# Sums written in the place of their low parts, a spare region in their stead, and two first images with orders of their own

## What is computed

```python
# x: 32 images, 256 channels, 28 x 28
xp  = log_pooling(x)                     # 12 averages over bins of a 9 x 9 neighbourhood, (2 levels x 6 angles)
out = conv(xp, w_conv1, stride=(4, 3))   # 256 -> 256 channels, one weight for each of the 12 averages
out = out + conv(x, w_center, 1 x 1) + b_center
mean, var = over images and places, per channel
out = (out - mean) * rsqrt(var + 1e-5) * gamma + beta
return relu(out + x)
```

## Time and profile before

| | us |
|---|---|
| median of 3 runs | 1634.29 |
| lowest, highest | 1633.83, 1634.32 |
| the profiled execution | 1634.39 |
| its span | 1632.7 |
| TensorE busy | 1459.9 (89%) |
| DVE busy | 1421.4 (87%) |
| ACT busy | 639.6 (39%) |
| GpSimd busy | 121.3 (7%) |
| data moved | 268.76 MB |

### The profile page before, as it was taken

The page is one execution under the profiler, slowest core; times in us unless marked ns, Lnnn a source line. Parts: engine busy times, 40 slices in busy tenths (PEclk is TensorE's granted clock), DMA queues, the critical chain, the costliest instruction groups (busy, mean ns, idle before and its releaser), DMA issues.

```text
span 1632.7 us, 22865 instructions
## 1 busy us (share of the span) xinstructions
PE 1459.9 (89%) x8468; PEld 1458.6 (89%) x8468; DVE 1421.4 (87%) x1391; ACT 639.6 (39%) x689; POOL 121.3 (7%) x160
## 2 busy tenths in 40 slices
PE   6899999999999999999999999999999999992000
PEld 5899999999999999999999999999999999992000
DVE  7999999999999999999999999999999999986332
ACT  3334434334334343443433334343343333435332
POOL 1000000000000000000000000000000000000000
PEclk8999999999999999999999999999999999996555
DMA  6456554555555555455545555555555455579999
GB/s 200 108 132 146 136 134 126 125 145 127 119 124 133 145 136 137 128 122 143 135 115 120 136 139 136 141 127 128 135 136 122 116 140 133 136 253 420 425 425 400
DMA packets 65352, 268.76 MB, mean 165 GB/s; under 512 B 7616, under 2 KB 7616, under 8 KB 65344
## 3 DMA queue, kind: packets, MB, share of 16 engines
q1 hardware_dynamic: 39744, 160.53, 29.5%
q0 software_dynamic: 20736, 82.45, 26.5%
q10 hardware_dynamic: 4864, 25.69, 3.8%
HBM read 218.07 MB, written 50.58 MB: 165 GB/s over the span
## 4 chain that ended last, share of the span: by engine, by line
PE 86%; DMA 6%; DVE 3%; ACT 2%; another core or an unknown queue 1%; issue 1%; ACTq 0%; SPq 0%; DVEq 0%; POOLq 0%
PE acc L676 29%; PE acc L677 29%; PE acc L675 29%; DMA out<-phase 3%; DMA phase<-y_dram 2%; ACT phase L444 1%; DMA row<-x_wide 1%; DVE pooled L452 1%; DVE pooled_split L453 1%; DVE inner_split L453 0%; ACTq L447 0%; ACT m_copy L403 0%; DVE y_stage L452 0%; DVE row3v L452 0%
## 5 line engine op out<-in xcount | busy, mean ns | idle before, releaser
L387 ACT ACTIVATE pooled_split<-pooled 128x1456 fp32r<-128x1456 f32 x192 | 273.4, 1424 | 609.6 <-DVE pooled L452 609.6
L453 DVE TENSOR_TENSOR pooled_split<-pooled,pooled_split 128x1456 fp32r<-128x1456 f32 x192 | 315.1, 1668 | 0.3 <-ACT pooled_split L387 0.3
L675 PE MATMUL acc<-pooled_split,w_first 128*128 128x364 f32 x768 | 252.7, 329 | 5.1 <-DVE pooled_split L453 5.1
L676 PE MATMUL acc<-pooled_split,w_first 128*128 128x364 f32 x768 | 253.4, 330 | 0.0
L677 PE MATMUL acc<-pooled_split,w_first 128*128 128x364 f32 x768 | 253.4, 330 | 0.0
L677 PE MATMUL acc<-pooled_split,w_outer 128*128 128x364 f32 x768 | 252.8, 329 | 0.0
L676 PE MATMUL acc<-pooled_split,w_outer 128*128 128x364 f32 x768 | 252.5, 329 | 0.0
L675 PE MATMUL acc<-pooled_split,w_outer 128*128 128x364 f32 x768 | 252.0, 328 | 0.0
L675 PE MATMUL acc<-inner_split,w_first 128*128 128x392 f32 (+1 forms) x640 | 219.2, 342 | 13.6 <-DVE inner_split L453 9.3
L677 PE MATMUL acc<-inner_split,w_first 128*128 128x392 f32 (+1 forms) x640 | 218.3, 341 | 0.0
L676 PE MATMUL acc<-inner_split,w_inner 128*128 128x392 f32 (+1 forms) x640 | 218.0, 341 | 0.0
(11 more groups left out here) (82 smaller groups left out, 2154.9 us busy)
## 6 DMA issues: line engine op xcount, KB each, us to landing
row<-x_wide SPq DMA_DIRECT2D x64, 558.0 KB, 3.6
row<-x_wide POOLq DMA_DIRECT2D x64, 558.0 KB, 7.3
ends<-x_wide SPq DMA_DIRECT2D x64, 504.0 KB, 4.0
ends<-x_wide POOLq DMA_DIRECT2D x64, 504.0 KB, 5.8
x_pad<-x SPq DMA_DIRECT2D x64, 392.0 KB, 3.1
y_dram<-y_stage SPq DMA_DIRECT2D x31, 784.0 KB, 8.5
phase<-y_dram SPq DMA_DIRECT2D x30, 784.0 KB, 30.8
out<-phase ACTq DMA_DIRECT2D x30, 784.0 KB, 34.4
```

The lines of the kernel that those rows point to most:

```text
L387: nc.scalar.activation(view(pooled_split, 2 * j * PAIR, (1, PAIR)), view(pooled, (PAIRS * c + j) % 2 * PAIR, (1, PAIR)), ACT.Copy)\
L453: sub = lambda out_, a, b: nc.vector.tensor_tensor(out_, a, b, ALU.subtract)
L675: nc.tensor.matmul(place, hi_w, hi_in, start=start, stop=False)
L676: nc.tensor.matmul(place, lo_w, hi_in, start=False, stop=False)
```

## The change

`inner` and `pooled` are given up. Their sums are written into `phase2` at `INNER_LOW` and `POOLED_LOW`, which are the low halves of `inner_split` and `pooled_split`, and the low part is taken in place. So DVE now waits, ahead of each sum, until TensorE has used the low part of the slice before (`pooled_place`, `inner_done`); ACT's waits for the same go. A region `spare` of the same size as the two buffers is put behind `w_stage`, so that all other buffers move and the total stays.

The first three places of phase two are fetched earlier: place 0 after image 29, places 1 and 2 after image 30. The places within `w_stage` and `spare` are 7 instead of 4, and those up to `w_first` 12 instead of 9. The load of the next x waits for the differences too.

DVE's order is now three: `first_image`, in which each group of weights stands just ahead of its use and each low part right behind its sum; `second_image`; and `image_steps` for the loop, in which columns and boxes come first, then the differences, two pooled sums, and only then the low parts of the inner sums. The warm-up has 70 matmuls.

```diff
--- before.py
+++ after.py
@@ -86,6 +86,8 @@
                 return phase1.enter_context(nc.sbuf_tensor(name, [P, size], dt))
 
             w_stage = reused("w_stage", CH * RAW * CHANNELS)
+
+            spare = reused("spare", 2 * PAIR + 4 * HALF)
             w_first = reused("w_first", 2 * TAPS * CHANNELS, F32R)
             row2 = reused("row2", (W + 3) * ROW2_H)
             row3 = reused("row3", (W + 2) * ROW3_H)
@@ -94,8 +96,6 @@
             box3 = reused("box3", (W + 2) * BOX3_H)
             ends = reused("ends", W * ENDS_H)
             d03 = reused("d03", 2 * U * TALL)
-            inner = reused("inner", 4 * HALF)
-            pooled = reused("pooled", 2 * PAIR)
             INNER = 6 * HALF
             inner_split = reused("inner_split", 2 * INNER, F32R)
             w_inner = reused("w_inner", 2 * INNER_TAPS * CHANNELS, F32R)
@@ -108,6 +108,9 @@
 
         D1, D2, VD, SD = 0, HALF, 2 * HALF, 4 * HALF
 
+        INNER_LOW = start_of["inner_split"] + INNER
+        POOLED_LOW = start_of["pooled_split"] + PAIR
+
         def w_part(c, lo, tap):
 
             if c == 0:
@@ -127,9 +130,9 @@
         def places_within(name):
             return end_of[name] // PLACE
 
-        AFTER_STAGE = places_within("w_stage")
+        AFTER_STAGE = places_within("spare")
         AFTER_FIRST = places_within("w_first")
-        AFTER_SUMS = places_within("pooled")
+        AFTER_SUMS = places_within("d03")
         AFTER_INNER = places_within("w_inner")
         AFTER_PAIR = (start_of["pooled_split"] + 2 * 2 * PAIR) // PLACE
         ALL_PLACES = 2 * (SLOTS - 1)
@@ -212,7 +215,7 @@
         relu_done = sem("relu_done")
         stored = [sem(f"stored{d}") for d in range(SLOTS)]
 
-        WARM_UP = 20
+        WARM_UP = 70
         KINDS = 2
         MOMENTS = KINDS * CH
 
@@ -292,16 +295,17 @@
                 wait_from_one(sp, pooled_ready, PAIRS * s)
                 begin_sum(image, c, ends, W, ends_begun)
 
-            def load_weights(c):
-                for part, (first, end) in enumerate(((0, RAW_OUTER), (RAW_OUTER, RAW))):
-                    sp.dma_start(view(w_stage, (c * RAW + first) * CHANNELS, (1, (end - first) * CHANNELS)),
-                                 w_raw[:, c, first:end, :].rearrange("p k o -> p (k o)"))\
-                        .then_inc(w_loaded[c][part], 16)
+            def load_weights(c, part):
+                first, end = ((0, RAW_OUTER), (RAW_OUTER, RAW))[part]
+                sp.dma_start(view(w_stage, (c * RAW + first) * CHANNELS, (1, (end - first) * CHANNELS)),
+                             w_raw[:, c, first:end, :].rearrange("p k o -> p (k o)"))\
+                    .then_inc(w_loaded[c][part], 16)
 
             def image_steps(image, first=False, last=False):
                 for c in range(CH):
                     if not last:
                         sp.wait_ge(row3_ready, CH * image + c + 1)
+                        sp.wait_ge(v_ready, CH * image + c + 1)
                         load_x(image + 1, c)
                     if c == 0:
                         begin_sums(image, 1)
@@ -324,20 +328,29 @@
                     (load_tail_x if k % 2 else load_tail_y)(0, 1 + k // 2)
 
             load_x(0, 0)
-            load_weights(0)
-            begin_sums(0, 0)
+            load_weights(0, 0)
+            begin_sum(0, 0, row2, W + 3, row2_begun)
+            load_weights(0, 1)
+            begin_sum(0, 0, ends, W, ends_begun)
             load_x(0, 1)
-            load_weights(1)
+            load_weights(1, 0)
+            load_weights(1, 1)
             for dst, src in ((bias, b_center), (gam, gamma), (bet, beta)):
                 sp.dma_start(dst[:, :], src).then_inc(params_loaded, 16)
             image_steps(0, first=True)
-            with sp.Fori(1, LAST) as image:
+            with sp.Fori(1, LAST - 2) as image:
                 image_steps(image)
+
+            image_steps(LAST - 2)
+            sp.wait_ge(w_lo_ready, CH * len(GROUPS))
+            sp.wait_ge(y_saved, 16 * (LAST - 3))
+            load_places(0, 1)
+            image_steps(LAST - 1)
+            load_places(1, 3)
             image_steps(LAST, last=True)
 
             sp.wait_ge(y_saved, 16 * LAST)
-            sp.wait_ge(w_lo_ready, CH * len(GROUPS))
-            load_places(0, AFTER_STAGE)
+            load_places(3, AFTER_STAGE)
             sp.wait_ge(pooled_done, PAIRS * (CH * IMAGES - 1))
             load_places(AFTER_STAGE, AFTER_FIRST)
             sp.wait_ge(pooled_lo_ready, PAIRS * CH * IMAGES)
@@ -373,19 +386,17 @@
 
             def split_inner(s):
                 act.wait_ge(v_ready, s + 1)
-                wait_from_one(act, inner_done, s)
-                nc.scalar.activation(view(inner_split, 0, (1, SD)), view(inner, 0, (1, SD)), ACT.Copy)\
+                nc.scalar.activation(view(inner_split, 0, (1, SD)), view(phase2, INNER_LOW, (1, SD)), ACT.Copy)\
                     .then_inc(inner_hi_ready, 1)
 
                 nc.scalar.activation(view(inner_split, SD, (HALF, 2), (H, U), (1, H)),
                                      view(d03, 2, (U * TALL - 2, 2), (TALL, U), (1, H)), ACT.Copy)\
                     .then_inc(inner_hi_ready, 1)
 
-            def split_pooled(s, c, j):
-                wait_from_one(act, pooled_done, PAIRS * s - PAIRS + j + 1)
+            def split_pooled(s, j):
                 act.wait_ge(pooled_ready, PAIRS * s + j + 1)
                 nc.scalar.activation(view(pooled_split, 2 * j * PAIR, (1, PAIR)),
-                                     view(pooled, (PAIRS * c + j) % 2 * PAIR, (1, PAIR)), ACT.Copy)\
+                                     view(phase2, POOLED_LOW + 2 * j * PAIR, (1, PAIR)), ACT.Copy)\
                     .then_inc(pooled_hi_ready, 1)
 
             def copy_m1(image):
@@ -413,19 +424,17 @@
                     split_inner(s)
                     if c == 1 and not first:
                         measure(image - 1, 1)
-                    if first and c == 0:
-                        split_weights(0, range(FIRST_OUTER_GROUP - 1, len(GROUPS)))
-                        split_weights(1, range(len(GROUPS)))
+                    if first:
+                        split_weights(c, range(len(GROUPS)))
                         act.wait_ge(warmed_up, 1)
                     for j in range(PAIRS):
-                        split_pooled(s, c, j)
+                        split_pooled(s, j)
                     if c == 0 and not first:
                         measure(image - 1, 0)
 
             act.wait_ge(zeroed, 1)
             nc.scalar.activation(std[:, :], std[:, :], ACT.Sqrt)
             act.wait_ge(zeroed, ZEROED)
-            split_weights(0, range(INNER_GROUPS))
             image_steps(0, first=True)
             with act.Fori(1, IMAGES) as image:
                 image_steps(image)
@@ -531,102 +540,157 @@
...
+            def pooled_place(s, j, first, *dims):
+                wait_from_one(dve, pooled_done, PAIRS * s - PAIRS + j + 1)
+                return view(phase2, POOLED_LOW + 2 * j * PAIR + first, *dims)
...
+                add(pooled_place(s, j, 0, (PAIR // 2, 2), (h, 2 * u), (1, h)),
...
+            def differences(image, c):
+                s = CH * image + c
+                dve.wait_ge(x_loaded[c], 16 * (image + 1))
+                wait_from_one(dve, inner_lo_ready, 2 * s)
...
+                wait_from_one(dve, inner_done, s)
+                add(view(phase2, INNER_LOW + D1, *striped), even, odd)
+                sub(view(phase2, INNER_LOW + D2, *striped), odd, even)
...
+            def three_columns(image, c):
+                s = CH * image + c
+                dve.wait_ge(x_loaded[c], 16 * (image + 1))
+                dve.wait_ge(row2_ready, 16 * (s + 1))
...
+            def first_image():
+
+                for c in range(CH):
+                    differences(0, c)
+                    transform_weights(c)
+                    lo_of_sums(c)
+                    lo_of_weights(c, range(INNER_GROUPS))
+                    lo_of_shifted(c)
+                    three_columns(0, c)
+                    boxes(c)
+                    first_sum(c)
+                    lo_of_weights(c, [FIRST_OUTER_GROUP - 1])
+                    lo_of_pooled(c, 0)
+                    second_sum(c)
+                    lo_of_weights(c, range(FIRST_OUTER_GROUP, len(GROUPS)))
+                    lo_of_pooled(c, 1)
+                    third_sum(c)
+                    lo_of_pooled(c, 2)
+
+            def second_image():
+
+                for c in range(CH):
+                    s = CH + c
+                    differences(1, c)
+                    if c == 0:
+                        take_middle(0)
+                    lo_of_sums(s)
+                    three_columns(1, c)
+                    if c == 0:
+                        take_y(0)
+                    lo_of_shifted(s)
+                    boxes(s)
+                    first_sum(s)
+                    lo_of_pooled(s, 0)
+                    second_sum(s)
```

(45 more changed lines are left out.)

90 lines of the change are left out of this document (43 added, 47 removed).

## The result

The changed kernel takes 1646.11 us (median, 1645.95 to 1646.98), the kernel before 1634.1 us on the same chip: a ratio of 1.0075 with an interval of 1.0057 to 1.0092. The forecast was 1645.3. The profiled execution has a span of 1644.4 us against 1632.7, so 11.7 us have to be found.

What follows compares the result with a forecast made beforehand. DVE was taken to bound the start, TensorE the loop at 22.63 us a slice, bytes the end phase. 1634.4 + 16.3 (start) - 5.7 (early places) + 0.3 (contention) = 1645.3 us, range 1639 to 1663.

Steps and rivals of the forecast that it cites:

- The loop stays at 22.63 us: Loop: TensorE's matmuls are unchanged, so each slice (half an image's channels) stays at 22.63 us, with 0.4 us of slack.
- The walk through images 0 and 1: DVE's first four slices, added step by step: done at 35.9, 65.7, 93.2 and 121.5 us, 11.7 us later than before.
- Row2 ahead of slice 4: Switch to the loop's order: DVE waits 0.9 us for row2, and TensorE starts slice 4 at 136.3 instead of 121.87.
- the term for the lower clock: Slice 4, after TensorE's gap: 3.4 us at the low clock level cost 1.5 us.
- The split of the loss: Start of the kernel: 9.8 us of loss from the switch to the loop's order, 4.6 from waits on ACT's copies.
- 70 warm-ups: Start: fifty more warm-up matmuls change nothing; TensorE's later waits for DVE cover their 0 to 0.7 us by slice 2.
- In place: DVE in the loop: taking the low part in place costs the same as from a separate buffer.
- Row2 in the loop: Loop: row2's accumulating half lands in about 7 us, within the 8.3 allowed, so no loss.
- The rival itself: Row2 lands too late in the loop, up to 17.5 us lost, 1663 or any part of it; chance 0.18.
- The end: End phase: three places fetched early gain 5.7 us; only bytes moved ahead count, other places coming free earlier bring nothing.
- the 0.3 for contention: Last image: early fetches compete with row2, costing 0 to 2 us, taken as 0.3.
- The other side: Rival: TensorE isn't held up before slice 4; full price 1628.7 us; chance 0.08 for faster, 0.04 for no change.

Runs made afterwards that it cites:

- the last experiment: Changed kernel with sums first in images 0 and 1, old loop order, image 1's take_y behind both sums, last y store ahead of ends: 1624.89 us, ratio 0.9942.

## Why the prediction was right, and where it was not

The time, the sign, the mechanism of the loss and its place came out as forecast (1646.1 against 1645.3). The two large terms were each too small, by 2.7 us (16.3 against 19.0) and by 1.9 (5.4 against 7.3), on opposite sides. That the sum is within 0.8 us is therefore in part luck. One attribution was wrong, of the loss to its two reorderings.

- **The loop stays at 22.63 us.** Right: 22.63, gapless, with the waits of DVE for TensorE ahead of the in-place sums. The slack was said to be 0.4 us; in the row at 704.44 the low part ends at 706.2 and the next slice starts at 186.08 + 23 x 22.633 = 706.65.
- **The walk through images 0 and 1.** DVE started at 4.2 (4.1 forecast), was through slice 0 at 37.7 (35.9), slice 1 at 67.6 (65.7), slice 2 at 95.0 (93.2) and slice 3 at 123.3 (121.5). The steps between them are 29.9, 27.4 and 28.4 against 29.8, 27.5 and 28.3. The whole error of 1.8 us is the landing of the first row2, taken at 17.3 and measured at 19.13, near the upper bound of 19.2 that the text gave.
- **Row2 ahead of slice 4.** The wait was 1.90 us, not 0.9. With the 1.8 from above, TensorE started slice 4 at 139.2 instead of 136.3. These 2.9 us are, within 0.2, the 2.7 by which the loss of TensorE (19.0) exceeds the 16.3 of the sum; the term for the lower clock, 1.5, was measured at 1.6.
- **The split of the loss.** Wrong as a cause. The text read 9.8 us for the switch and 4.6 for the copies off the time at which TensorE would have been ready. The runs give 13.6 to 17.9 for the copies and 3.9 to 8.2 for the switch. The step that failed: the text compared DVE's and TensorE's times at one point, slice 3, instead of walking once more with one part undone. TensorE's own lateness in slices 1 to 3 was caused by DVE too, so it was no given.
- **70 warm-ups.** Right: nothing (the run with 20 is the same), and the cover was the one named, since TensorE waits for DVE again later.
- **In place.** Right: the low part takes 1.67 us in place, as in the earlier trace rows, and no slice of the loop got longer.
- **Row2 in the loop.** Right on the verdict, and on the reason: the accumulating half lands 5.8 us after its issue (5.5 to 7.2), below the 7.3 of the earlier trace rows and below the 7 us taken. The Trainium skill, "DMA: Bandwidth & Descriptors", Anatomy of one DMA, would give an estimate of 3.3 us; no run here shows it. The rival itself was under-priced: 17.5 us by the landing bound, 70 us where a transfer of 784 KB pushed the loop there.
- **The end.** The sum had -5.7 + 0.3 = -5.4, measured -7.3, and the reasoning was half wrong. The text said that only bytes moved ahead count, and that the other places coming free earlier brings nothing. The early fetch was worth 4.2 us, not 5.7, and without the spare region nothing at all (the kernel before with early fetch alone); so spare is a necessary part. Against the 0.3 for contention, 3.1 us came from a source that was not in the sum: the new order leaves the y store 5.8 us to land instead of 8.5, and so the first fetch comes 33.7 us ahead of TensorE's end instead of 31.8. From 50 to 21 us ahead of TensorE's end the kernel before moves 210 GB/s and the run without the early fetch 239, which is 0.84 MB more, or 2.0 us at 417 GB/s. So about two thirds of the 3.1 us are won before w_first is free, which fits the earlier fetch; the rest was not separated from places released sooner by the new sizes. That a sooner first fetch pays is seen in the last experiment (2.3 us).
- **The other side.** The rival in which TensorE isn't held at the switch did not happen in the changed kernel, but the order of the low parts decides it: slice 4 at 124.5 and 1631.8 us with it undone, just above the 124.3 from which the text lets the gain of the end prevail by 0.2%. With the switch undone too the time is 1628.4, against the full price of 1628.7; but there 2.9 us come from TensorE ending sooner, which that price did not have, and less from the end.

## What to carry to other kernels

When an engine writes a result, another copies it, and the first needs the copy back, put one more piece of independent work between the two: here its absence cost twelve waits, eight of them of 1.5 us, and moved the end by 14 us, in a part of the run where that engine is the bound. To find what a reordering costs, walk the engine's order once with each part undone; do not split the loss by the time at which a consumer would have been ready, for that consumer was held by the same engine. And before fetching early, draw the gates of the destinations: a fetch that is moved ahead pays only if another is ready to take the place it leaves.

## What the runs showed of the hardware

- **A transfer issued one place earlier in its queue did not bring its follower forward.** The first half of row2 was moved ahead of a weight transfer of 768 KB. GpSimd could begin the accumulating half at 8.91 instead of 10.17, but this took 10.1 us to land instead of 9.0, so that DVE had its row at 19.13, against 19.21 in the earlier trace rows. In both kernels the DMA engines move 309 GB/s over the first 20 us; that all the bytes under way set the landing fits this, but no run isolates it.
- **The landing of an accumulating transfer goes with what is issued within a few us of it.** The 558 KB issued at 714.60 before, with the ends 0.5 us and the y store 1.1 us behind them, took 8.9 us. Those issued at 731.65 after, with the same two 3.1 and 3.7 us behind, took 5.8, and in the run with one extra transfer, at 716.40 with 0.6 and 1.1 us, 7.6. The medians of all 58, in which two kinds of places are mixed, are 7.3 before and 5.8 after. The y store beside it goes from 8.5 to 5.8 us.
- **A second disturbance cost nothing beyond the first.** One extra transfer of 784 KB an image and two cost the same, 2.3 to 2.4 us an image (one run each).
- **Subtracting in place is not slower.** The low part of the sums takes 1.78 us, in place or from a buffer of its own (1.78 in the earlier trace rows).
